# Up and gate projections as one Strassen-Winograd level over pairs of batches, in a fused gated-attention and ternary-FFN block

## The chip, the cores and the metric

The kernel runs on one core of one Trainium2 chip. The metric is device time in microseconds (us) of one execution. The kernel before takes 458.07 us (median of 3 runs, 457.31 to 458.22).

## What is computed

For each of 4 batches of 512 rows (model width 512): a layer norm of x is mixed by an attention matrix computed from a context of width 256, scaled by tanh of a gate and added to x; then a second layer norm feeds a gated FFN of width 2048 whose three weight matrices are made ternary.

```python
def ternary_quant(w):
    scale = jnp.mean(jnp.abs(w)) + EPS
    q = jnp.clip(jnp.round(w / scale), -1.0, 1.0) * scale
    return w + jax.lax.stop_gradient(q - w)
up = jnp.einsum('bsd,ed->bse', x, wu)          # wu, wg, wd: ternary
gate = jnp.einsum('bsd,ed->bse', x, wg)
hidden = jax.nn.silu(up) * gate
return jnp.einsum('bse,de->bsd', hidden, wd)
...
x = x + jnp.tanh(g_xattn[0]) * _L0_xattn_ref(_layernorm(x, axis=-1), ctx_1024, ...)
x = x + jnp.tanh(g_ffn[0]) * _L0_ffn_ref(_layernorm(x, axis=-1), W_up, W_gate, W_down)
```

## The kernel before, in words

One program drives six instruction streams, ordered by hand with semaphores. TensorE (`pe`), VectorE (`dve`), ScalarE (`act`), GpSimd (`pool`) and the DMA queue of SyncE (`sp`) each have a block; GpSimd also issues the loads of x.

**Attention, batches 0 to 3.** Per batch b: `project` (L303) makes q and k, `energy` (L312) the scores, the softmax runs on DVE and ACT, `transpose_p` (L322) turns the probabilities round, `mix` (L334, 8 fp32 matmuls a tile of 128 rows, 4 tiles) applies them, `make_x1` (L632) adds the result into x on DVE. Then `stats2`, `aggregate2`, a reciprocal root on GpSimd (`rstd2`, L256 and L259) and `norm_x1` (L647) give the second norm; `transpose_x` (L343) transposes it, ACT keeps the fp16 high part (`high_x`, L509), DVE the fp16 rest (`low_x`, L653). The stages of batch b+1 are interleaved with those of batch b by hand. Before the mix ACT adds a per-row shift to x (`shift_x`, L505).

**Weights.** `sum_abs` (L469) and `sum_abs_gate` (L474) on ACT sum the absolute values, `total` (L350) adds them over the partitions on PE, `weight_scale` (L661 to L667) on DVE makes the threshold; PE waits for it (`s_thr`) between batch 0 and batch 1. Two DVE operations make a piece ternary: `is_below` (L672) and `is_above_less` (L675). Up is done in batches 1 and 2 of the attention, gate and down tile by tile in the first FFN batch.

**FFN.** Batch after batch, over 16 tiles e of 128 hidden units. `up_gate` (L412 with the high part, L413 with the low) issues 2 x 4 x 2 = 16 matmuls of 128x512: up and gate, 4 blocks of the model width, high and low part. ACT makes silu (L579), DVE multiplies (`make_h`, L771), ACT takes the fp16 high part (L589), DVE the low (`low_h`, L776). `down` (L427, L428) issues 4 x 2 = 8 matmuls a tile, accumulating over e in four PSUM banks; L809 on DVE scales them, adds x, and `sp` stores. So the FFN is 4 x 16 x 16 = 1024 matmuls of up and gate and 4 x 16 x 8 = 512 of down.

```python
for k in range(KD):
    w = t_ug[:, ds(e * (KD * P) + (m * WCOLS + k * P), P)]
    pe.matmul(ps[par][:, :], w, hi[:, k, :], start=(k == 0), stop=False)
    last = pe.matmul(ps[par][:, :], w, lo[:, k, :], start=False, stop=(k == KD - 1))
```

## Time and profile before

| | |
|---|---|
| median of 3 runs | 458.07 us |
| the profiled execution | 458.36 us, its span 456.6 us |
| PE busy | 439.3 us (96% of the span), 1878 matmuls |
| DVE, ACT, POOL busy | 222.9, 162.4, 47.2 us |
| mean granted TensorE clock | 0.99 of full speed |

The span is from the first to the last instruction on the core. Matmuls are pipelined and the ends shown are modelled, so neighbouring matmuls overlap in the record: the distance from start to start is what one costs, not its duration. "Idle before" with a releaser names what an engine waited for. GpSimd is called POOL, TensorE PE, VectorE DVE, ScalarE ACT.

### The profile page before, as it was taken

How to read it: one execution, taken by the hardware profiler on the slowest of the kernel's cores; microseconds unless marked ns; L12 is line 12 of the kernel's file. 1: busy time of each engine (PE TensorE's matmuls, PEld its weight loads, DVE VectorE, ACT ScalarE, POOL GpSimd, SP SyncE). 2: the span in 40 equal slices, each digit the busy share in tenths (PEclk: the TensorE clock that was granted, in tenths of full speed). 3: DMA queues.
4: the chain of work that ended last, by engine and by line, in shares of the span. 5: the costliest groups of instructions: out<-in, count | busy, mean ns of one | idle time of the engine just before them, and what ended most of it. 6: DMA issues, size and time to landing. Idle time of an engine off the chain costs nothing.

```text
span 456.6 us, 6607 instructions
## 1 busy us (share of the span) xinstructions
PE 439.3 (96%) x1878; PEld 204.7 (45%) x1878; DVE 222.9 (49%) x384; ACT 162.4 (36%) x264; POOL 47.2 (10%) x115
## 2 busy tenths in 40 slices
PE   7995999999799999999999999999999999999996
PEld 5443444544344444444444444444444444444442
DVE  0576299998787767745222232422332252322224
ACT  2794577766522222222222222222222222222221
POOL 1225045446200000000000000000000000000000
PEclk9999899999989999999999999999999999999999
DMA  7997413332000000002000000200000011000002
GB/s 260 392 420 286 162 46 126 133 134 92 1 2 0 0 0 0 0 0 92 1 0 0 0 0 1 92 0 0 0 0 0 0 46 48 0 0 0 0 0 92
DMA packets 8445, 27.68 MB, mean 61 GB/s; under 512 B 1136, under 2 KB 1136, under 8 KB 6896
## 3 DMA queue, kind: packets, MB, share of 16 engines
q1 hardware_dynamic: 7344, 23.34, 13.8%
q0 software_dynamic: 1088, 4.19, 2.4%
q8 instruction: 5, 0.08, 0.1%
q14 instruction: 8, 0.07, 0.0%
...
## 4 chain that ended last, share of the span: by engine, by line
PE 85%; DVE 6%; issue 4%; POOL 2%; ACT 1%; DVEq 1%; POOLq 0%; ACTq 0%
PE bank L412 24%; PE bank L413 24%; PE bank L427 12%; PE bank L428 12%; PE bank L334 5%; PE bank L303 3%; PE bank L312 2%; POOL r L259 1%; DVE x_sb L632 1%; DVE st L637 1%; PE bank L322 1%; PE bank L355 1%; PE bank L343 1%; DVE t_ug L675 0%; DVE below L672 0%
## 5 line engine op out<-in xcount | busy, mean ns | idle before, releaser
L412 PE MATMUL bank<-xh,t_ug 128*128 128x512 f16 (+1 forms) x512 | 194.7, 380 | 0.0
L413 PE MATMUL bank<-xl,t_ug 128*128 128x512 f16 (+1 forms) x512 | 194.6, 380 | 0.0
L771 DVE SCALAR_TENSOR_TENSOR shared<-shared,kap,bank 128x512 f32<-128x512 f32 x64 | 47.8, 747 | 133.4 <-PE bank L413 133.2
L427 PE MATMUL bank<-shared 128*128 (+1 forms) x256 | 97.4, 381 | 3.0 <-DVE shared L776 3.0
L428 PE MATMUL bank<-shared 128*128 (+1 forms) x256 | 97.5, 381 | 0.0
L579 ACT ACTIVATE shared<-bank,su 128x512 f32<-128x512 f32 x64 | 44.0, 687 | 118.2 <-PE bank L413 118.2
L589 ACT ACTIVATE shared<-shared 128x512 f16<-128x512 f32 x64 | 40.3, 629 | 126.2 <-DVE shared L771 123.5
L412 PEld LDWEIGHTS bank<-xh,t_ug 128*128 (+1 forms) x512 | 50.3, 98 | 60.7 <-issue 1.0
L413 PEld LDWEIGHTS bank<-xl,t_ug 128*128 (+1 forms) x512 | 50.3, 98 | 60.6 <-issue 0.8
L776 DVE TENSOR_TENSOR shared<-shared 128x512 f16<-128x512 f32 x64 | 44.3, 692 | 54.0 <-ACT shared L589 54.0
L334 PE MATMUL bank<-shared,xt_sb 128*128 128x512 f32 (+1 forms) x128 | 57.5, 593 | 0.2 <-ACT shared L498 0.2
L427 PEld LDWEIGHTS bank<-shared 128*128 128x128 f16 x256 | 25.1, 98 | 33.4 <-DVE shared L675 3.0
L428 PEld LDWEIGHTS bank<-shared 128*128 128x128 f16 x256 | 25.1, 98 | 30.1 <-issue 0.3
L334 PEld LDWEIGHTS bank<-shared,xt_sb 128*128 128x128 f32 x128 | 23.3, 190 | 24.9 <-issue 23.9
L675 DVE SCALAR_TENSOR_TENSOR t_ug<-w_st,thr,below 128x512 bf16 (+2 forms) x24 | 22.3, 928 | 2.6 <-DVE below L672 2.2
L672 DVE TENSOR_SCALAR below<-w_st,nthr 128x512 bf16 (+2 forms) x40 | 21.4, 534 | 0.3 <-DVE nthr L667 0.2
L303 PE MATMUL bank<-shared,wqk 128*128 128x512 f32 x32 | 17.7, 687 | 2.8 <-DVE nthr L667 2.8
L612 DVE TENSOR_REDUCE nmax<-bank 128x1 f32<-128x512 f32 x16 | 11.0, 687 | 12.5 <-PE bank L312 12.4
L312 PE MATMUL bank<-shared 128*128 128x512 f32 x32 | 15.5, 596 | 0.8 <-ACT shared L481 0.8
L488 ACT ACTIVATE shared<-bank,nmax 128x512 f32<-128x512 f32 x16 | 11.0, 685 | 13.9 <-DVE nmax L612 13.6
L632 DVE SCALAR_TENSOR_TENSOR x_sb<-bank,tr,x_sb 128x512 f32<-128x512 f32 (+1 forms) x16 | 12.0, 747 | 8.0 <-PE bank L334 6.6
L653 DVE TENSOR_TENSOR xl<-bank,xh 128x512 f16<-128x512 f32 (+1 forms) x16 | 11.0, 688 | 8.1 <-ACT xh L509 7.8
...
## 6 DMA issues: line engine op xcount, KB each, us to landing
...
bqk_sb<-in_bqk SPq DMA_DIRECT2D x1, 1.0 KB, 3.3
```

The costliest lines, as they stand in the source:

```text
L303: last = pe.matmul((ps_q, ps_k)[m][:, :], wqk[:, c, m, :], ctx_sb[:, c * ROWS:(c + 1) * ROWS], start=(c == 0), stop=(c == NC - 1))
L312: pe.matmul(e_bank(b, i), q_sb[:, i * P:(i + 1) * P], k_sb, start=True, stop=True).then_inc(s_e, 1)
L334: last = pe.matmul(ps_x[i % 2][:, :], xt_sb[:, i, k, :], at[:, k, :], start=(k == 0), stop=(k == KD - 1))
L412: pe.matmul(ps[par][:, :], w, hi[:, k, :], start=(k == 0), stop=False)
L413: last = pe.matmul(ps[par][:, :], w, lo[:, k, :], start=False, stop=(k == KD - 1))
L427: pe.matmul(ps_o[j][:, :], hh[par][:, j * P:(j + 1) * P], w, start=first, stop=False)
L428: ins = pe.matmul(ps_o[j][:, :], hl[par][:, j * P:(j + 1) * P], w, start=False, stop=last)
L579: act.activation(a_sb[par], ps_up[par][:, :], ACT.Silu, scale=su[:, :]).then_inc(s_a, 1)
L589: act.activation(hh[par], h_sb[par], ACT.Copy).then_inc(s_hh, 1)
L675: dve.scalar_tensor_tensor(dst, w_st[:, ds(at, n)], thr[:, m:m + 1], tmp, ALU.is_gt, ALU.subtract).then_inc(done, 1)
L771: dve.scalar_tensor_tensor(h_sb[par], a_sb[par], kap[:, :], ps_gate[par][:, :], ALU.mult, ALU.mult).then_inc(s_h, 1)
L776: dve.tensor_tensor(hl[par], h_sb[par], hh[par], ALU.subtract).then_inc(s_hl, 1)
```

## The change

The 16 tiles of hidden units become 8 units of two tiles (rows 1 and 2 of a 2x2 block matrix A, whose columns are the two halves of the model width), for up and gate alike. The other factor B is a 2x2 block matrix too: its rows are the halves of the model width, its columns the two batches of a pair (0 and 1, then 2 and 3). `n` runs over 16 pairs of unit and batch pair. One Strassen-Winograd level replaces the eight block products by seven (`product1` to `product7`), each of 2 x 2 x 2 = 8 matmuls of 128x512, into PSUM pairs of banks (up beside gate).

- **Block sums of the weights** (S1 to S4, `unit_sums`) are made on POOL, four operations of 128x512 bf16 a unit. POOL also makes units 2 to 7 ternary (`unit_ternary`, three operations of 128x1024 for up and three for gate) and does the "below" half for units 0 and 1, whose other half is on DVE. The ternary values and the sums lie over the staged weights.
- **Block sums of the activations** (T1 to T4): the transposed norm is kept in fp32 (`xf`, `copy_x` in place of `high_x`/`low_x`), summed by operations of 128x1024 on DVE and POOL, and each of the seven blocks is then split in fp16 high (`high_t`, ACT) and low (`low_t`, DVE), 128x1024 at a time. For the second pair POOL makes the sums after the last unit of weights, and the splits are done in units 6 to 8.
- **Recombination**: a unit needs three copies from PSUM on ACT (`copy_1`, `copy_u2`, `copy_5`, 128x1024) and three adds on DVE (`add_11`, `add_12`, `add_22`, 128x1024); two of the products accumulate upon others in PSUM.
- **Down** (`down_half`, `expand`): from n = 3 to 14 one batch of one two-unit group is expanded between product 3 and product 7, 32 matmuls, with four evictions that add into x; the last four units (n = 12 to 15) close in eight banks at the end. There are 512 down matmuls as before, and 12 x 4 + 8 = 56 evictions of 128x512 where there were 16.
- **x of batches 2 and 3** is stored to a DRAM buffer after `make_x1` (8 stores), its place holds the ternary down weights, and it is loaded again over batches 0 and 1 once these are stored. Down weights are loaded twice (for the mean, then again in four pieces after the attention), and made ternary on DVE at n = 1, 3, 4 and 5 (`ternary_down`).
- **Attention**: `shift_x` leaves it (the shift is added on ACT at n = 4, 5, 12, 13); up's and gate's scale is computed together in batch 2, so that PE no longer waits for a threshold between batches 0 and 1; POOL's two small chains have the operations named above between them. x is loaded from the `sp` queue. The hardware loops are unrolled. `XS` goes from 2^10 to 2^8.

```diff
 @block.gpsimd
+            def unit_ternary(m, u):
...
+                pool.tensor_scalar(below[0][:, :], w_unit(m, u), nthr[:, m:m + 1], None, ALU.is_lt)\
+                    .then_inc(s_belp, 1)
+                pool.tensor_scalar(below[1][:, :], w_unit(m, u), thr[:, m:m + 1], None, ALU.is_gt)\
+                    .then_inc(s_belp, 1)
+                hold(pool, s_belp, 2 * k + 2)
+                pool.tensor_tensor(a_unit(m, u), below[1][:, :], below[0][:, :], ALU.subtract).then_inc(s_ternp, 1)
+            def unit_sums(u):
...
+                pool.tensor_tensor(a_blk(u, S1), a_blk(u, A21), a_blk(u, A22), ALU.add).then_inc(s_sum, 1)
+                hold(pool, s_sum, 4 * u + 1)
+                pool.tensor_tensor(a_blk(u, S2), a_blk(u, S1), a_blk(u, A11), ALU.subtract).then_inc(s_sum, 1)
+                hold(pool, s_sum, 4 * u + 2)
+                pool.tensor_tensor(a_blk(u, S4), a_blk(u, A12), a_blk(u, S2), ALU.subtract).then_inc(s_sum, 1)
+                pool.tensor_tensor(a_blk(u, S3), a_blk(u, A11), a_blk(u, A21), ALU.subtract).then_inc(s_sum, 1)
+            for b in range(NB):
                 for i in range(NT):
-                    rstd2(b, i, final=last and i == NT - 1)
+                    rstd2(b, i)
...
+                    if b == 2 and i in (1, 2):
+                        unit_below(i - 1, 0)
+                    if b == 3 and i == 0:
...
+                        pool.tensor_tensor(xf_half(0, 0), xf_half(1, 1), xf_half(0, 0), ALU.add).then_inc(s_t2, 1)
+                    if b == 3 and i == 1:
...
+                        pool.tensor_tensor(xf_half(0, 1), xf_half(0, 1), xf_half(0, 0), ALU.subtract).then_inc(s_t4, 1)
+                    if b == 3 and i == 2:
+                        unit_below(0, 1)
+                        unit_below(1, 1)
+            unit_sums(0)
+            unit_sums(1)
+            unit_ternary(0, 2)
+            unit_ternary(1, 2)
+            unit_sums(2)
...
+            for u in range(3, NU):
+                unit_ternary(0, u)
+                unit_ternary(1, u)
+                unit_sums(u)
...
 @block.tensor
+            def product(n, j, dst, a, blk, start):
...
+                for m in range(2):
+                    for k in range(2):
+                        w = a_unit(m, u) if a < 4 else wbf[:, m, u * 2 * UC + UC:(u + 1) * 2 * UC]
+                        o = (a % 4) * 256 + k * P
+                        pe.matmul(dst[:, m * 512:(m + 1) * 512], w[:, o:o + P], hi[:, k * 512:(k + 1) * 512],
+                                  start=start and k == 0, stop=False, skip_group_check=not start)
+                        last = pe.matmul(dst[:, m * 512:(m + 1) * 512], w[:, o:o + P], lo[:, k * 512:(k + 1) * 512],
+                                         start=False, stop=k == 1, skip_group_check=not start)
+            def product1(n):
+                if n < NU:
...
+                        pe.wait_ge(s_ternp, 2 * (n - 2) + 2)
...
+            for n in range(NN - 1):
+                product6(n)
+                product3(n)
...
+                if n >= 3:
+                    down_half(n)
+                product7(n)
+                product1(n + 1)
+                product2(n + 1)
+                product5(n + 1)
+                product4(n)
...
 @block.vector
+            for n in range(NN):
+                down = 3 <= n < NN - 1
+                low_h(n, "11")
+                if n > 0:
+                    make_h(n - 1, "21")
+                    low_h(n - 1, "21")
+                add_12(n)
+                if down:
+                    evict_half(n, 0)
+                make_h(n, "12")
...
+                low_h(n, "12")
+                add_22(n)
+                make_h(n, "22")
+                if n + 1 < NN:
+                    add_11(n + 1)
+                low_h(n, "22")
+                if n + 1 < NN:
+                    make_h(n + 1, "11")
```

On ACT, a unit is: `high_h(n, "11")`, `silu(n-1, "21")`, `copy_u2(n)`, `high_h(n-1, "21")`, `silu(n, "12")`, `high_h(n, "12")`, `silu(n, "22")`, `copy_1(n+1)`, `high_h(n, "22")`, `silu(n+1, "11")`, `copy_5(n+1)`. Product 6 waits for `copy_1`, product 3 for `copy_5`, product 7 for `copy_u2`; product 2 of the next unit waits for `add_11`, product 5 for `add_12`, product 4 for `add_22`.

## Rows read from the trace of the kernel before

**Rows 1.** The page: busy time, and POOL over 40 equal slices.
```profile
PE 439.3 (96%) x1878; PEld 204.7 (45%) x1878; DVE 222.9 (49%) x384; ACT 162.4 (36%) x264; POOL 47.2 (10%) x115
...
POOL 1225045446200000000000000000000000000000
```
**Rows 2.** Stages: length, busy us (x instructions) of each engine, clock, DMA share, GB/s.
```profile
39.70:44.50 4.80, 0.36 (x2) 0.30 (x2) 3.28 (x10) 1.61 (x2) 2.74 (x7) 1.00 0.61 227
44.50:92.00 47.50, 46.58 (x148) 23.05 (x148) 36.70 (x69) 32.50 (x62) 17.98 (x38) 0.96 0.35 116
92.00:113.90 21.90, 20.81 (x66) 10.14 (x67) 19.91 (x42) 13.50 (x21) 11.98 (x29) 1.00 0.30 109
113.90:130.40 16.50, 12.85 (x58) 6.02 (x57) 12.71 (x27) 7.55 (x11) 3.32 (x7) 0.90 0.00 0
130.40:453.00 322.60, 321.90 (x1492) 145.70 (x1490) 130.39 (x194) 81.62 (x124) 0.00 (x0) 1.00 0.03 10
```
**Rows 3.** Timeline of PE around its waits: start us, us, instruction, [idle before].
```profile
41.46 0.36 PE L350 MATMUL bank<-wabs,ones 128*128 128x4 f32 x2 [1.82 <-ACT t_ug L469]
44.56 3.51 PE L303 MATMUL bank<-shared,wqk 128*128 128x512 f32 x4 [2.75 <-DVE nthr L667]
...
113.94 0.38 PE L412 MATMUL bank<-xh,t_ug 128*128 128x512 f16 x1
...
125.84 0.38 PE L427 MATMUL bank<-shared 128*128 128x512 bf16 x1 [2.96 <-DVE shared L776]
```
**Rows 4.** FFN matmuls: groups of the page, and one later stage.
```profile
L412 PE MATMUL bank<-xh,t_ug 128*128 128x512 f16 (+1 forms) x512 | 194.7, 380 | 0.0
...
L427 PE MATMUL bank<-shared 128*128 (+1 forms) x256 | 97.4, 381 | 3.0 <-DVE shared L776 3.0
...
200.00:260.00 60.00, 60.00 (x279) 27.20 (x278) 19.90 (x28) 15.11 (x23) 0.00 (x0) 1.00 0.05 18
```
**Rows 5.** Groups by line and shape: busy us, mean ns of one, idle before.
```profile
L771 DVE SCALAR_TENSOR_TENSOR shared<-shared,kap,bank 128x512 f32<-128x512 f32 x64 | 47.8, 747 | 133.4 <-PE bank L413 133.2 <-issue 0.2
L776 DVE TENSOR_TENSOR shared<-shared 128x512 f16<-128x512 f32 x64 | 44.3, 692 | 54.0 <-ACT shared L589 54.0
L579 ACT ACTIVATE shared<-bank,su 128x512 f32<-128x512 f32 x64 | 44.0, 687 | 118.2 <-PE bank L413 118.2
L589 ACT ACTIVATE shared<-shared 128x512 f16<-128x512 f32 x64 | 40.3, 629 | 126.2 <-DVE shared L771 123.5 <-PE bank L428 2.7
L675 DVE SCALAR_TENSOR_TENSOR t_ug<-w_st,thr,below 128x1024 bf16 x8 | 10.2, 1279 | 0.0
L474 ACT ACTIVATE t_ug<-w_st x8 | 8.3, 1048 | 0.0
L469 ACT ACTIVATE t_ug<-w_st 128x2048 bf16<-128x2048 f32 x4 | 7.6, 1900 | 0.0
L672 DVE TENSOR_SCALAR below<-w_st,nthr 128x1024 bf16 x8 | 6.0, 747 | 0.0
```
**Rows 6.** Groups on POOL, by shape.
```profile
L226 POOL TENSOR_SCALAR_AFFINE_SELECT ident<-ident 128x128 f32<-128x128 f32 x1 | 0.3, 287 | 0.0
L285 POOL TENSOR_SCALAR kap<-scale 128x1 f32<-128x1 f32 x1 | 0.2, 190 | 0.0
```
**Rows 7.** Timeline of DVE (first row) and POOL: the same POOL operation beside it and alone.
```profile
60.15 1.28 DVE L675 SCALAR_TENSOR_TENSOR t_ug<-w_st,thr,below 128x1024 bf16 x1
...
60.78 0.69 POOL L247 TENSOR_TENSOR tr<-r,tanh_sb 128x1 f32<-128x1 f32 x1
61.65 0.26 POOL L249 TENSOR_SCALAR km<-mv,tr 128x1 f32<-128x1 f32 x1 [0.18 <-POOL tr L247]
...
79.04 0.19 POOL L247 TENSOR_TENSOR tr<-r,tanh_sb 128x1 f32<-128x1 f32 x1
```
**Rows 8.** Timeline of the end.
```profile
451.92 0.38 PE L428 MATMUL bank<-shared 128*128 128x512 bf16 x1
452.06 2.31 SPq L208 DMA_DIRECT2D out<-x_sb  x4
```

More of the change, by code:

```diff
@@ L315, in transpose_p @@
                 pe.wait_ge(s_pn, b * NT + i + 1)
[L316 removed]
+                if b > 0:
                     pe.wait_ge(s_at, b * NT + i)
@@ L363, in _ @@
                 transpose_p(0, i)
-            def attention(b, first=False, last=False):
+            for b in range(NB):
+                first, last = b == 0, b == NB - 1
                 if not (first or last):
@@ new lines, in product4, with expand @@
+            def product4(n):
+                pe.wait_ge(s_c["22"], n + 1)
+                product(n, 4, ps_c[n % 2], A22, "T4", False)
+            def expand(dst, units, b, i, first, last):
+                for n in units:
+                    for r in range(2):
+                        c = ("11", "21")[r] if b % 2 == 0 else ("12", "22")[r]
+                        pe.wait_ge(s_lo[c], n + 1)
+                        e = 2 * (n % NU) + r
+                        pe.wait_ge(s_td, e // 2 + 1)
+                        for lo in range(2):
+                            ins = pe.matmul(dst, h_part(n, c, lo)[:, i * P:(i + 1) * P], t_d[:, e * DM:(e + 1) * DM],
+                                            start=first and n == units[0] and r == 0 and lo == 0,
+                                            stop=last and n == units[-1] and r == 1 and lo == 1)
+                if last:
+                    ins.then_inc(s_dt, 1)
@@ L520, in _ @@
                 copy_at(0, i)
-            def attention(b, first=False, last=False):
+            for b in range(NB):
+                first, last = b == 0, b == NB - 1
                 if not last:
@@ L567, in _ @@
-            attention(0, first=True)
-            for c in range(NABS):
-                act.wait_ge(d_w[1][c], 16)
-            with act.Fori(1, NB - 1) as b:
-                attention(b)
-            attention(NB - 1, last=True)
-            high_x(NB - 1, NT - 2, NB * NT - 2)
-            def silu(b, e, par, head=False):
-                act.wait_ge(s_up, b * NE + e + 1)
-                if not head:
-                    act.wait_ge(s_h, b * NE + e - 1)
-                act.activation(a_sb[par], ps_up[par][:, :], ACT.Silu, scale=su[:, :]).then_inc(s_a, 1)
@@ L608, in _ @@
+            silu(NN - 1, "21")
+            high_h(NN - 1, "21")
         @block.vector
@@ L818 @@
+            make_h(NN - 1, "21")
+            low_h(NN - 1, "21")
+            for t in range(8):
+                b, i = (3, t) if t < 4 else (2, t - 4)
+                evict(4 * LAST_D + t, (bank[2:6] + [bank[0], bank[1], bank[6], bank[7]])[t], b, i)
 def kernel(x, ctx_1024, g_xattn, g_ffn, L0_xattn_Wq, L0_xattn_bq, L0_xattn_Wk, L0_xattn_bk,
```

1020 lines of the change are left out of this document (613 added, 407 removed).

## The prediction

> **What bounds the kernel now.** I read the page's busy line first: PE is busy 96% of the span, DVE 49%, ACT 36%, POOL 10% and over by the middle of the span [rows 1]. Then the table by stages, because the mean hides two different halves. From 130.4 to 453.0 us PE is busy 321.9 of 322.6 us at full clock, while DVE works 130 us and ACT 82; before that PE has small holes, and DVE is nearly full (19.9 of 21.9 us before the FFN) [rows 2]. So two thirds of the time is a stream of matmuls that waits for nobody, and only fewer matmuls shorten it. The durations shown for matmuls (380 ns) are modelled; 279 of them start in 60 us of a later stage, so one costs 60/279 = 0.215 us [rows 4]. There is something to win in the holes too: PE idles from 39.7 to 44.5 us for the first threshold, and waits 2.96 us at 122.9 us for the down weights [rows 2, 3]; the stage around that (16.5 us) has a granted clock of 0.90, about 1.6 us more.
>
> **Part 1, the matmuls.** Up and gate go from 1024 matmuls to 16 x 7 x 8 = 896; down keeps 512. 128 x 0.215 = **27.6 us** less, all on PE's path [rows 4]. One unit is 56 x 0.2155 = 12.1 us of PE, with half a down group (32 matmuls, 6.9 us) 19.0 us.
>
> **Part 2, the holes of the attention.** The 4.8 us stage goes, as nothing else in it was late for PE (ctx of batch 2 is loaded long before), and with it the slow clock behind it: 0.96 over 47.5 us is 1.9 us [rows 2, 3]. The down threshold is made in batch 3, which takes away the 2.96 us and the slow stretch behind it, 1.6 us [rows 2, 3]. What is late next: ACT. In batch 1 it gets eight pieces of work of its own: six sums of 128x2048 at 1.9 us where there were four of 1.05 [rows 5], and two splits of 128x1024 (about 1.05 us each), against four shifts that leave. That is 6 x 2.1 + 2.1 - 4 x 1.25 - 4 x 0.6 = 7.3 us more, on an engine that was busy 32.5 of 47.5 us [rows 2]: 16 of 24 us a batch become 23.6. Walking through the order, `copy_at` behind the sums reaches the transposes and the first mix of batch 2 about 3 us late. DVE is relieved in the same stages (eight pairs L672/L675 of 2.0 us leave it) [rows 5]. POOL's small chains now have large operations between them, and in batch 3 the roots of tiles 1 and 2 come behind one addition of 128x1024 each; DVE's `norm_x1` and with it `make_x1` of the last tile wait. I take 3 us (between 0 and 6). Sum: 4.8 + 1.9 + 3.0 + 1.6 - 3 - 3 = **5.3 us** less.
>
> Without any stall in the FFN that makes 458.4 - 27.6 - 5.3 = 425.5 us. The FFN's own small waits of before (0.7 and 0.6 us at the transposes, part of the 0.90 clock) also go: about 1.4 more, but the first unit has one of 1 us, for `product5(0)` needs the last root (3 us after the last mix) and then one sum on POOL. Base: **425 us**. The tail is as before: last matmul, one eviction, one store of 2.3 us [rows 8].
>
> **Part 3, the recombination: hidden if DVE and ACT are alone.** Per unit DVE gets three adds of 128x1024 from PSUM (1.28, by L675, the same form), four `make_h` (0.75), four `low_h` (0.69) and from n = 3 four evictions (0.75) [rows 5]: 9.6 and 12.6 us against 12.1 and 19.0 of PE. ACT gets three copies (1.05 by L474), four silu (0.69) and four copies (0.63): 8.4 us [rows 5]. The tightest link is `copy_u2`: product 7 waits for it, and in units without a down half only product 3 (1.72 us) lies between; 1.05 plus a wait fits. `make_h(n-1, "21")` must be done when the down half starts, 3.5 us after product 4 ended: silu 0.69 and 0.75 fit. So units 8 to 14, where POOL has no more work, should run as a closed stream. That is where half of the 27.6 us is safe. Unhidden are units 6 to 8, with seven more splits on ACT (1.05) and DVE (1.28) in the middle of the order: 2 us. The DRAM round trip of x has a unit of 19 us in between and costs PE nothing.
>
> **Part 4, POOL.** This is the open term. POOL has shown no large operation. Its work per unit 2 to 7 is four comparisons and two subtractions of 128x1024 and four sums of 128x512. Bounds: the 128x128 select took 287 ns and a 128x1 operation 190, so 0.8 ns an element in one pass [rows 6]. Lower end: every operation is one pass, 1.0 us for 1024 and 0.6 for 512: 8.4 us a unit. Upper end: two-input operations are three passes (2.65 and 1.4 us), comparisons two (1.8): 18.1. I take two passes for two inputs (1.8 and 1.0) and one for a comparison, nearest to the row: 4 x 1.0 + 2 x 1.8 + 4 x 1.0 = 11.6 us. Nine waits at 0.15 to 0.18 us [rows 7] make it 12.9.
>
> POOL also shares something with DVE: an operation on 128x1 took 0.69 us beside DVE's L675 (two SBUF inputs), ending 0.04 us after it, and 0.19 us alone [rows 7]. If the large ones behave so, POOL stands while DVE runs an operation with two SBUF inputs: `low_h` and three `make_h`, 5.0 us a unit, and 4.1 more (two pairs L672/L675) at n = 1, 3, 4 and 5.
>
> With product 1 of unit 0 at time 0 and POOL free at 3 us: sums of units 0 and 1 are done at 14.5; ternary of unit 2 at 28, while PE wants it at 24.3 (**late 4**); its sums 34.5, three small coefficients 36; ternary of unit 3 at 48, PE is there at 40 (**late 8**); unit 4 at 66 and PE at 67; later ones are ahead. Sum 12 us, and the clock: the two waits of the trace each cost 1.6 to 1.9 us of slow clock [rows 2], so 2 us more. DVE waits for POOL in turn; if it waits half a POOL operation (0.5 us) at each of 7 to 11 shared operations, units 3 to 5 have 16.7 + 5 us of DVE against 19 of PE, less 1.5 us by which neighbouring DVE operations overlap: 5 us. Part 4: **19 us**. With 2 us of part 3: 425 + 21 = 446; but the waits of PE in units 2 and 3 give DVE and ACT back the time in which they are late, so I take off 3: **443 us**, 3.3% under the median of 458.07 (the sum stands on the profiled 458.36, 0.3 us higher).
>
> The Trainium skill bears on this in two places, which the sum does not use. "SBUF — State Buffer" (Who interferes with whom) says that the port pair shared by VectorE and GpSimd is an exclusive lock for the whole instruction; the 0.69 us beside DVE agrees for one direction, the other no row shows. "GPSIMD Engine Reference" (Elementwise — side-by-side cycle accounting) gives 4497 ns for a two-input add of 2048 fp32, so an estimate of 2.3 us for 1024; with it the lateness of unit 3 would be some 16 instead of 12 us and the time about 450. It speaks against putting this work on POOL.
>
> **Rivals.**
> *Everything hidden.* POOL makes its operations in one pass (9.7 us a unit with waits), and DVE does not disturb it: unit 2 is ready at 19, before 24.3, and nothing is late. 425 + 2 = 427, or 421 if the attention gives back its 6 us too. For it: 0.8 ns an element [rows 6]. Against it: two inputs, and rows 7.
> *Slower: POOL is the pace of the first half.* Its place are units 2 to 7, its price the upper end: 18.1 + 1.3 + about 7 us of DVE's shared operations = 26.4 us a unit against 19.0. Then unit 2 is 11 us late, unit 3 27, unit 4 33, units 5 to 7 7.4 each more: 55 us; 425 + 55 + 2 + 3 = 485. It decides from 33 us of stalls (458 - 425), which is a POOL unit of some 17 us before DVE's share. For it: PE, DVE and POOL are coupled by one order, and a late comparison delays seven products. A milder one (20 us a unit) gives 463.
> *The links inside a unit.* If silu, multiply, split and add run in each other's way so that each of 16 units loses 0.7 us, the second half shows it too: 443 + 11 = 454. For it: DVE has 9.6 of 12.1 us in units 0 to 2; against it: 12.6 of 19.0 later.
>
> **How the numbers follow.** The forecast (431 to 453) 0.48; everything hidden (below 431) 0.19; links (453 to 457.1) 0.06; slower by POOL 0.24; what is left, 0.03, is no change. A difference of 0.2% (0.9 us) is about what a measurement of this kernel can tell from none. Faster by more: 0.48 + 0.19 + 0.06 = 0.73, minus 0.01 for the edge: 0.72; within: 0.04; slower: 0.24. The time is that of the likeliest case, 443; the range for 8 in 10 is 422 to 467: it takes in the lower case and the milder slower one, and leaves out the 485. The forecast's own range is 431 to 453.
>
> **What would show it.** L412's successors: 896 matmuls; from unit 8 on PE full, with units of 19.0 us. Right in part 4: PE waits for POOL before product 1 of units 2 and 3, none later; POOL's 128x1024 subtractions near 1.8 us, sums near 1.0. Wrong: PE waiting for POOL at every unit to 7 (slower), or never (hidden). Right in part 2: no wait of 2.75 us between batches 0 and 1, first FFN matmul near 113 us (113.9 before); wrong if it starts after 117 or before 109. If PE waits for DVE or ACT in units 9 to 14, part 3 is wrong. DVE's operations with two SBUF inputs longer than 1.28 and 0.69 us beside POOL would show the coupling in the other direction.

## The result, and the profile after

The kernel after takes 483.03 us (median of 4 runs, 481.19 to 483.66) against 458.14 us (457.31 to 458.49, 4 runs): a ratio of 1.054, 95% interval 1.051 to 1.057. The profiled execution is one of 483.66 us, its span 481.8. The prediction was 443, range 422 to 467, and wrong in sign.

The page of the kernel after: busy time, POOL over 40 slices, granted clock, and the groups of POOL's large operations and of DVE's operations with two SBUF inputs (busy us, mean ns of one, idle before).

```profile
PE 424.2 (88%) x1733; PEld 193.2 (40%) x1748; DVE 314.3 (65%) x408; ACT 218.1 (45%) x318; POOL 217.1 (45%) x189
...
POOL 0233354878999999999999952000000000000000
PEclk9999999998698869979797999999999999999999
...
L1031 DVE SCALAR_TENSOR_TENSOR xf<-xf,small 128x512 f32<-128x512 f32 x48 | 41.9, 872 | 22.8 <-ACT xf L792 22.2
L1036 DVE TENSOR_TENSOR sh<-xf,sh 128x512 f16<-128x512 f32 x48 | 38.2, 797 | 14.6 <-ACT sh L798 14.5
...
L343 POOL TENSOR_SCALAR below<-w_sb,small 128x1024 bf16<-128x1024 f32 x12 | 36.5, 3043 | 1.0 <-POOL w_sb L348 1.0
L345 POOL TENSOR_SCALAR below<-w_sb,small 128x1024 bf16<-128x1024 f32 x12 | 35.5, 2958 | 0.0
...
L348 POOL TENSOR_TENSOR w_sb<-below 128x1024 bf16<-128x1024 bf16 x12 | 27.4, 2286 | 1.8
```

POOL, over by the middle of the span and 10% busy before [rows 1], is a row of nines from the 11th to the 23rd slice, and PE's clock has its gaps in the same slices. A comparison takes 3.0 us, a subtraction 2.3. The stages of the kernel after (length, busy us and instructions of PE, PEld, DVE, ACT and POOL, clock, DMA share, GB/s):

```profile
39.70:44.50 4.80, 4.80 (x18) 2.51 (x18) 2.45 (x6) 2.83 (x7) 2.30 (x7) 1.00 0.80 284
...
109.00:130.40 21.40, 10.88 (x44) 5.16 (x45) 15.17 (x19) 4.91 (x6) 19.50 (x17) 0.76 0.22 74
130.40:200.00 69.60, 53.53 (x216) 22.21 (x215) 48.73 (x47) 27.29 (x38) 66.87 (x33) 0.88 0.05 16
200.00:260.00 60.00, 44.83 (x178) 18.39 (x181) 46.33 (x43) 20.77 (x30) 57.77 (x27) 0.87 0.10 36
260.00:320.00 60.00, 57.43 (x254) 25.18 (x256) 44.65 (x51) 30.05 (x40) 25.41 (x12) 0.96 0.00 1
320.00:380.00 60.00, 59.84 (x277) 27.20 (x278) 38.67 (x48) 24.49 (x35) 0.00 (x0) 1.00 0.21 71
```

The second half is what was forecast: PE full, 277 matmuls in 60 us. In the first half POOL is busy 144.1 of 151.0 us (109.0 to 260.0), while PE stands still for a quarter of it and issues at a lower clock. The stage of the old threshold wait (39.7 to 44.5), where PE had 0.36 us of work [rows 2], is full now.

The waits of PE that cost most, from its timeline (start us, us, instruction, [idle before <- what ended it]):

```profile
123.62 0.58 PE L524 MATMUL pair<-xb_hi,w_sb 128*128 128x512 f16 x1 [10.27 <-issue]
124.00 0.63 PE L526 MATMUL pair<-xb_lo,w_sb 128*128 128x512 f16 x1
124.43 0.63 PE L524 MATMUL pair<-xb_hi,w_sb 128*128 128x512 f16 x1
...
151.08 0.39 PE L524 MATMUL pair<-xb_hi,w_sb 128*128 128x512 f16 x1 [2.38 <-POOL w_sb L348]
...
176.72 0.61 PE L524 MATMUL pair<-xb_hi,w_sb 128*128 128x512 f16 x1 [7.27 <-POOL w_sb L348]
...
204.28 0.59 PE L524 MATMUL pair<-xb_hi,w_sb 128*128 128x512 f16 x1 [5.60 <-DVE x_sb L1066]
...
232.79 0.59 PE L524 MATMUL pair<-xb_hi,w_sb 128*128 128x512 f16 x1 [5.03 <-DVE x_sb L1066]
```

Three different causes stand here. At 123.62 us it is product 5 of the first unit, which waits for its block sum (POOL ends it at 123.52). At 151.08 and 176.72 us it is product 1 of units 2 and 3, whose weights are not yet ternary. At 204.28 and 232.79 us it is product 1 of n = 4 and 5, and at 258.65 us that of n = 6 (4.45 us), which wait for an eviction on DVE; POOL had made their weights ternary 5.5, 9.9 and 12.2 us before. Behind the waits of 10.27, 7.27 and 5.03 us the granted clock is 0.50, and matmuls start 0.43 us apart instead of 0.215, the lower of the two clock levels (1.2 GHz).

**Losses by unit.** I take the start of each unit's second product (of the first product for n = 0) from the timeline, and subtract the unit's length without stalls (12.1 us for n < 3, 19.0 later). The starts are 109.7, 135.8, 153.9, 180.1, 207.7, 236.2, 262.0, 282.2, 303.9, 322.9, so the losses of n = 0 to 7 are 14.0, 6.0, 14.1, 8.6, 9.5, 6.8, 1.2 and 2.7: 62.9 us, and nothing later. Without them the kernel would take 109.7 + 3 x 12.1 + 12 x 19.0 + 44.9 (unit 15 to the end of the span) + 1.9 = 420.8 us. The waits over 0.25 us in these units add up to 43.8 us; the other 19 are the lower clock behind them, smaller gaps, and some 1.4 us of two transposes that stand in unit 0.

### The profile page after: what moved, and what is told of

Same layout as the page of the kernel before. It is cut to its first block, busy times and chain, and to the rows that moved or that the text cites. A ratio compares the mean times of both kernels' runs of the same rounds, so it can differ in the third digit from the quotient of the medians.

```text
span 481.8 us, 5521 instructions
## 1 busy us (share of the span) xinstructions
PE 424.2 (88%) x1733; PEld 193.2 (40%) x1748; DVE 314.3 (65%) x408; ACT 218.1 (45%) x318; POOL 217.1 (45%) x189
## 4 chain that ended last, share of the span: by engine, by line
PE 62%; POOL 16%; DVE 9%; issue 8%; ACT 4%; DMA 1%; POOLq 0%; DVEq 0%; ACTq 0%
PE pair L595 19%; PE pair L524 15%; PE pair L526 15%; PE pair L453 6%; PE pair L423 3%; POOL below L343 2%; POOL below L345 2%; POOL w_sb L348 2%; POOL below L333 2%; PE pair L432 2%; DVE t_tmp L1050 2%; DVE x_sb L1052 1%; DVE x_sb L1066 1%; POOL small L324 1%; DMA sh<-in_ctxT 1%
## 5 line engine op out<-in xcount | busy, mean ns | idle before, releaser
L524 PE MATMUL pair<-xb_hi,w_sb 128*128 128x512 f16 x448 | 179.3, 400 | 42.8 <-DVE x_sb L1066 15.1
L526 PE MATMUL pair<-xb_lo,w_sb 128*128 128x512 f16 x448 | 178.9, 399 | 0.0
L595 PE MATMUL pair<-x_sb,sh 128*128 128x512 bf16 x497 | 110.6, 379 | 3.5 <-DVE x_sb L1066 1.6
L524 PEld LDWEIGHTS pair<-xb_hi,w_sb 128*128 128x128 bf16 x448 | 45.8, 102 | 105.4 <-issue 38.7
L595 PEld LDWEIGHTS pair<-x_sb,sh 128*128 128x128 f16 x512 | 49.5, 98 | 64.4 <-DVE x_sb L1066 4.6
L526 PEld LDWEIGHTS pair<-xb_lo,w_sb 128*128 128x128 bf16 x448 | 45.6, 102 | 56.7 <-issue 9.8
L1066 DVE SCALAR_TENSOR_TENSOR x_sb<-pair,small,x_sb 128x512 f32<-128x512 f32 x56 | 41.8, 747 | 32.6 <-PE pair L595 31.5
L453 PE MATMUL pair<-sh,xt_sb 128*128 128x512 f32 x128 | 57.5, 593 | 0.1
L1031 DVE SCALAR_TENSOR_TENSOR xf<-xf,small 128x512 f32<-128x512 f32 x48 | 41.9, 872 | 22.8 <-ACT xf L792 22.2
L1036 DVE TENSOR_TENSOR sh<-xf,sh 128x512 f16<-128x512 f32 x48 | 38.2, 797 | 14.6 <-ACT sh L798 14.5
L343 POOL TENSOR_SCALAR below<-w_sb,small 128x1024 bf16<-128x1024 f32 x12 | 36.5, 3043 | 1.0 <-POOL w_sb L348 1.0
L345 POOL TENSOR_SCALAR below<-w_sb,small 128x1024 bf16<-128x1024 f32 x12 | 35.5, 2958 | 0.0
L1036 DVE TENSOR_TENSOR sh<-c,sh 128x512 f16<-128x512 f32 x16 | 14.1, 882 | 21.8 <-ACT sh L798 21.8
```

What stands on the lines that cost most here:

```text
L343: pool.tensor_scalar(below[0][:, :], w_unit(m, u), nthr[:, m:m + 1], None, ALU.is_lt)\
L345: pool.tensor_scalar(below[1][:, :], w_unit(m, u), thr[:, m:m + 1], None, ALU.is_gt)\
L453: last = pe.matmul(ps_x[i % 2], xt_tile(i)[:, k, :], at[:, k, :], start=(k == 0), stop=(k == KD - 1))
L524: pe.matmul(dst[:, m * 512:(m + 1) * 512], w[:, o:o + P], hi[:, k * 512:(k + 1) * 512], start=start and k == 0, stop=False, skip_group_che ...
L526: last = pe.matmul(dst[:, m * 512:(m + 1) * 512], w[:, o:o + P], lo[:, k * 512:(k + 1) * 512], start=False, stop=k == 1, skip_group_check= ...
L595: ins = pe.matmul(dst, h_part(n, c, lo)[:, i * P:(i + 1) * P], t_d[:, e * DM:(e + 1) * DM], start=first and n == units[0] and r == 0 and l ...
```

## The experiments

Losses of n = 0 to 7 in the same manner, for the kernels that matter below (the first four compute everything, the last three leave POOL's weight operations out):

| kernel | us | losses of n = 0 to 7 | sum |
|---|---|---|---|
| after | 483.0 | 14.0, 6.0, 14.1, 8.6, 9.5, 6.8, 1.2, 2.7 | 62.9 |
| h1_fast_ternary | 473.8 | 14.0, 1.4, 11.1, 10.4, 7.5, 4.6, 1.3, 2.7 | 53.0 |
| f4_all_mended | 465.5 | 14.2, 0, 7.7, 8.6, 4.7, 0.5, 0.4, 9.9 | 46.0 |
| f5_sums_on_dve | 462.0 | 14.5, 0, 7.5, 8.6, 4.8, 0.4, 0.5, 5.6 | 41.9 |
| e1_pool_free | 450.9 | 11.1, 0, 4.9, 4.6, 3.7, 4.7, 0, 2.6 | 31.6 |
| k1_pool_free_mended | 447.9 | 12.0, 0, 2.1, 2.9, 0.5, 0.4, 0.5, 11.4 | 29.8 |
| k2_floor_sums_on_dve | 443.2 | 11.8, 0, 2.1, 2.9, 0.4, 0.5, 0.4, 5.7 | 23.8 |

### POOL's weight operations taken away

```diff
-pool.tensor_scalar(below[0][:, :], w_unit(m, u), nthr[:, m:m + 1], None, ALU.is_lt)
-pool.tensor_scalar(below[1][:, :], w_unit(m, u), thr[:, m:m + 1], None, ALU.is_gt)
-pool.tensor_tensor(a_unit(m, u), below[1][:, :], below[0][:, :], ALU.subtract)
+pool.memset(w_unit(m, u), 0.0)
...
-(the four block sums of a unit)
+pool.memset(a_blk(u, blk), 0.0)  # u < 2, a nop for the others
```

> Leaves out GpSimd's work on the up and gate weights: its comparisons, subtractions and block sums are replaced by memsets of zeros over the same places (one of 128x1024 fp32 for a unit and matrix, four small ones for units 0 and 1); all of PE, ACT and DVE stays. Theory P (POOL's work, by its own length and by what it does to DVE beside it, is what makes the changed kernel slow): the first FFN product stays near 109 us, then 1408 x 0.2155 = 303 us follow nearly closed, plus a few us in units 0 and 6 to 8 and 4 us of tail: 418 to 428 us. Theory R (the recombination chain of ACT and DVE, with 120 us more of DVE and ACT work, costs PE by itself): PE's waits in the first half stay at more than half of their 65 us: 450 to 470 us.

Measured: 450.94 us (450.33 to 451.83), ratio 0.987 (0.985 to 0.989). POOL's weight work costs 32 us: the losses halve, from 62.9 to 31.6, and the first FFN matmul starts 2.2 us earlier (107.5). Theory P (418 to 428) is refuted as the whole cause; the time lies at the lower end of theory R's range.

### Is it POOL's lateness, or what POOL reads?

```diff
-(the two comparisons)
+for r in range(6): pool.memset(below[r // 3][:, :], 0.0)   # each with its wait
```

> GpSimd's two comparisons of each unit and matrix (units 2 to 7), 2.9 us each beside DVE, are each replaced by three write-only memsets of 128x1024 bf16 with a wait behind each (about 3 x 0.95 + 0.2 us); the result of the comparison is left out. So POOL is as late as before, but reads nothing for two thirds of its time. Theory P1 (POOL's lateness is the cost): PE still gets a unit each 22 us or later, 470 to 482 us. Theory P2 (POOL's reads stop DVE's operations with two SBUF inputs and the chain evict, product 1 pays): DVE's operations go back to 0.75 and 0.69 us, PE's waits for evictions go, only those for POOL in units 2 and 3 stay: 450 to 462 us.

Measured: 485.52 us, ratio 1.062 (1.060 to 1.064). Six memsets of 0.96 us, which read nothing, cost as much as two comparisons of 3.0. It is above the ranges of both theories (470 to 482 and 450 to 462). So it is not the reading of the comparisons that costs. The run does not part POOL's time from its reading altogether: it leaves the comparisons out, but keeps subtraction and sums, which read, and these are what POOL does beside DVE's down weights in n = 3 and 4. The four operations in front of the last eviction of n = 4 take 1.78, 1.99, 1.45 and 1.98 us here, as long as in the kernel after (below).

### The down weights' ternary on DVE taken away

```diff
-dve.tensor_scalar(t_tmp, part, nthr[:, 2:3], None, ALU.is_lt)
-dve.scalar_tensor_tensor(t_d[...], part, thr[:, 2:3], t_tmp, ALU.is_gt, ALU.subtract)
+dve.memset(x_sb[:, o:o + 512], 0.0)
```

> Leaves out the ternary form of the down weights on DVE at n = 1, 3, 4 and 5 (eight pairs of 1.3 and 2.0 us in the changed kernel), memsets of 128x512 fp32 stand in its place. Theory P1: POOL paces the first half, its unit still takes 20.2 us of operations and waits, DVE was only late because it had time: 475 to 483 us (POOL is disturbed a little less). Theory P2 (DVE paces units 3 to 5): the 5 us waits of product 1 of units 4, 5 and 6 for the last eviction go: 463 to 470 us.

Measured: 473.2 us, ratio 1.035 (1.032 to 1.037); the down weights are left out. This is between the two theories. The waits for an eviction in n = 3 to 5 are gone, and waits of 3.2, 3.0 and 0.7 us for POOL appear in their place; the one for POOL at unit 3 grows from 7.3 to 9.3 us, and unit 7 loses 9.9 us instead of 2.7. So behind DVE's block POOL is the next limit of these units. In the kernel after, DVE's timeline shows the mechanism: between the third and the last eviction of n = 4 stand four operations, stretched by POOL, and product 1 of n = 5 starts 0.88 us after that last eviction began.

```profile
223.35 1.40 DVE L1066 SCALAR_TENSOR_TENSOR x_sb<-pair,small,x_sb 128x512 f32<-128x512 f32 x2
224.67 1.61 DVE L1050 TENSOR_SCALAR t_tmp<-xt_sb,small 128x1024 bf16<-128x1024 f32 x1
226.38 1.99 DVE L1052 SCALAR_TENSOR_TENSOR x_sb<-xt_sb,small,t_tmp 128x1024 bf16<-128x1024 f32 x1
228.48 1.45 DVE L1050 TENSOR_SCALAR t_tmp<-xt_sb,small 128x1024 bf16<-128x1024 f32 x1
230.03 1.95 DVE L1052 SCALAR_TENSOR_TENSOR x_sb<-xt_sb,small,t_tmp 128x1024 bf16<-128x1024 f32 x1
231.91 0.74 DVE L1066 SCALAR_TENSOR_TENSOR x_sb<-pair,small,x_sb 128x512 f32<-128x512 f32 x1
```

### POOL's prices by themselves

A kernel of single operations (POOL alone, then ten DVE operations beside four pairs of POOL's); it computes nothing of the reference.

> Computes nothing of the block; it measures single operations. First GpSimd alone, each operation twice with a wait behind it: if the comparison of 128x1024 fp32 is slow by itself it takes 2.8 us alone, and if its output type or the comparison is the reason, multiply and add or minimum and maximum on the same tile take 0.9 to 1.5 us; if every pass over fp32 costs that, they take 2.8 too. The two-input bf16 subtraction 2.1 us, 512 columns 1.15. Then GpSimd comparisons and two-input subtractions beside one kind of DVE operation at a time. Theory P2: DVE's operation with two SBUF inputs and its fp32 tensor_scalar (0.75 alone) are stretched by up to a whole GpSimd operation, the one with a PSUM and one SBUF input is not; beside GpSimd memsets the two-input one is not stretched.

Groups of POOL: L129 is the comparison beside DVE and L48 the same alone, L111 one with a constant, L60 and L66 two-input operations, L96 and L84 multiply and add.

```profile
L129 POOL TENSOR_SCALAR B<-xs,thr 128x1024 bf16<-128x1024 f32 x4 | 14.8, 3696 | 1.4 <-DVE D L176 0.9 <-POOL F L132 0.5
...
L48 POOL TENSOR_SCALAR B<-xs,thr 128x1024 bf16<-128x1024 f32 x1 | 2.8, 2844 | 4.5 <-DVE D L174 4.5
...
L111 POOL TENSOR_SCALAR B<-xs 128x1024 bf16<-128x1024 f32 x1 | 2.8, 2767 | 0.2 <-POOL B L108 0.2
...
L60 POOL TENSOR_TENSOR B<-B 128x1024 bf16<-128x1024 bf16 x1 | 2.1, 2114 | 0.1
...
L66 POOL TENSOR_TENSOR B<-B 128x512 bf16<-128x512 bf16 x1 | 1.1, 1148 | 0.1
...
L96 POOL TENSOR_SCALAR F<-xs,thr 128x1024 f32<-128x1024 f32 x1 | 1.1, 1118 | 0.2 <-POOL F L93 0.2
...
L84 POOL TENSOR_SCALAR F<-xs 128x1024 f32<-128x1024 f32 x1 | 1.0, 1044 | 0.2 <-POOL F L81 0.2
```

Groups of DVE: x10 beside POOL's comparison and two-input operation, x8 beside its memsets, x1 alone.

```profile
L179 DVE SCALAR_TENSOR_TENSOR D<-xs,thr,D 128x1024 bf16<-128x1024 f32 x10 | 20.5, 2051 | 1.0
L186 DVE TENSOR_SCALAR D<-xs,thr 128x1024 bf16<-128x1024 f32 x10 | 17.8, 1776 | 1.1
L193 DVE TENSOR_TENSOR D<-ps,xs 128x1024 bf16<-128x1024 f32 x10 | 12.3, 1225 | 1.0
L200 DVE SCALAR_TENSOR_TENSOR D<-xs,thr,D 128x1024 bf16<-128x1024 f32 x8 | 10.3, 1284 | 0.8
L165 DVE SCALAR_TENSOR_TENSOR D<-xs,thr,D 128x1024 bf16<-128x1024 f32 x1 | 1.3, 1285 | 12.5 <-POOL thr L44 12.5
L168 DVE TENSOR_SCALAR D<-xs,thr 128x1024 bf16<-128x1024 f32 x1 | 0.8, 753 | 0.1
```

A comparison is 2.84 us, but multiply and add (L84, L96) 1.04 to 1.12. Both engines stretch: POOL's comparison from 2.84 to 3.70, DVE's two-input operation from 1.28 to 2.05, its fp32 one-input operation from 0.75 to 1.78. DVE's operation with one operand in PSUM stays at 1.23, and POOL's memsets do not stretch the two-input operation (the only one run beside them).

### Another arithmetic on POOL

The prices suggest rounding by adding a large constant in place of comparing. Two versions: the first uses subtract with min, and max with multiply.

```diff
+pool.tensor_scalar(w_unit(m, u), w_unit(m, u), inv[:, m:m + 1], RND, ALU.mult, ALU.add)
+pool.tensor_scalar(below[0][:, :], w_unit(m, u), RND, 1.0, ALU.subtract, ALU.min)
+pool.tensor_scalar(a_unit(m, u), below[0][:, :], -1.0, 1.0, ALU.max, ALU.mult)
```

> One part changed: GpSimd makes a piece of units 2 to 7 ternary without comparisons, in three arithmetic passes (times 1/scale plus 1.5 x 2^23, which rounds; minus it and min 1; max -1), by the single-operation run 1.12 + 1.04 + 1.04 us with 0.17 us waits, where two comparisons and a subtraction took 2.84 + 2.84 + 2.11. A unit on POOL falls from 20.2 to about 12.6 us of operations and waits, 17 us beside DVE: no longer the pace. What is left is what the run with POOL freed left. Theory P and D together: 451 to 458 us. If POOL's length was not what mattered (only its contention, which stays), 470 or more.

Measured: 485.76 us, ratio 1.061 (1.059 to 1.063), a miss: in this trace the first pass takes 1.19 us, the others 3.70 and 3.83. For subtract with min only the pair can be the reason, as min with max took 1.04 us in m1 with the same input and output types; the pass with max and multiply also has another input type (bf16). The second version keeps to the pairs measured fast:

```diff
+pool.tensor_scalar(w_unit(m, u), w_unit(m, u), inv[:, m:m + 1], RND, ALU.mult, ALU.add)
+pool.tensor_scalar(w_unit(m, u), w_unit(m, u), RND + 1.0, RND - 1.0, ALU.min, ALU.max)
+pool.tensor_scalar(a_unit(m, u), w_unit(m, u), 1.0, -RND, ALU.mult, ALU.add)
```

> One part changed against the changed kernel: the ternary form of units 2 to 7 on POOL in three passes that use only operation pairs measured at 1.04 to 1.12 us for 128x1024 by themselves (multiply and add; min and max; multiply and add), where the earlier arithmetic form had two pairs (subtract and min; max and multiply) that took 3.9 and 3.7 us. POOL's unit then is 2 x 3.7 + 4.6 + 0.6 = 12.6 us before DVE's share, about 17 with it. Theory P: POOL is no longer the pace, and what stays is near the run with POOL freed (451): 451 to 459 us. If POOL's contention and not its length is the cost: 470 or more.

Measured: 473.79 us (473.33 to 475.05), ratio 1.035 (1.033 to 1.037). The passes take 1.47, 1.20 and 1.32 us; POOL's twelve weight blocks start from 135.9 to 214.0 us, 14.2 us a unit instead of 23.1 (134.4 to 261.3). The gain is 9 us, well short of the 32 of e1, and the time lies in the range given for "contention and not length" (470 or more). POOL's unit is now near the 12.9 us of the prediction, and the kernel still takes 31 us more than predicted. The 7.27 us wait for POOL's weights at unit 3 is gone, but in n = 2 PE waits 8.13 us for DVE's `add_22`: DVE stays stretched, as its groups from 130 to 235 us show (`make_h` and `low_h`, 0.75 and 0.69 without POOL [rows 5]).

```profile
L1036 DVE SCALAR_TENSOR_TENSOR xf<-xf,small 128x512 f32<-128x512 f32 x15 | 15.5, 1033 | 8.1 <-ACT xf L797 8.1
L1041 DVE TENSOR_TENSOR sh<-xf,sh 128x512 f16<-128x512 f32 x15 | 14.9, 990 | 5.4 <-ACT sh L803 5.4
```

### The order on DVE, and the first unit

g2_down_spread makes the down weights ternary piece by piece over n = 1 to 6 instead of two at once; f2 joins it with f1's arithmetic, and f3 adds a first attempt at the first unit (T2 and T4 a tile later, the below halves of units 0 and 1 on DVE).

> One part changed: the eight pieces of the ternary down weights on DVE are spread one by one over n = 1 to 6 (two at n = 3 and 6, the second one behind add_11), in place of pairs at n = 1, 3, 4, 5 in front of the last eviction; POOL as in the changed kernel. Theory D alone (DVE's block in front of the eviction is the cost of units 3 to 5): 463 to 468 us. Theory P and D together, as in the run without this work: POOL takes over as the pace, 472 to 479 us.

> Both parts: arithmetic ternary on POOL and the down pieces spread on DVE. Theory P and D together: the gain is larger than the sum of the two alone, since each hides the other; waits of product 1 for evictions and for POOL go, those in the first unit and at units 7 and 8 (about 10 and 3 us) stay: 436 to 444 us. If the links inside a unit cost (theory R): above 450.

> As the run before, and the start of the FFN mended: DVE makes the 'below' half of units 0 and 1 itself (POOL needed 2.9 us for each of four), and POOL's two additions for T2 and T4 come one tile later in batch 3, where its chains of reciprocal roots have room; the splits of T2 and T4 follow them. The 10 us wait of product 5 of unit 0 for the first block sum falls to 1 to 4 us: 6 to 9 us under the run before, 428 to 437 us. If that wait comes from DVE's or ACT's load at the end of the attention and not from POOL, within 2 us of the run before.

Measured: 480.28 (ratio 1.049, 1.047 to 1.051), 485.8 and 482.4 us. f2 and f3 carry f1's slow passes and are more than 40 us above their ranges. Spreading alone gives 3 us, less than either theory gave: the waits in n = 3 to 5 shrink, but n = 7 loses 10.6 us instead of 2.7 (units start at 271.1 and 300.7).

f4_all_mended is h1's arithmetic, the spreading, T2 and T4 and the below halves of units 0 and 1 on DVE, and the first unit's S1 and S2 ahead of the last root.

> All mended together: the fast ternary form on POOL, the down pieces spread over n = 1 to 6 on DVE, units 0 and 1 and the sums T2 and T4 on DVE, and the first two block sums of unit 0 before the last reciprocal root. Theory P and D: no wait over 3 us is left but one at n = 7; 1408 x 0.2155 = 303 us of FFN after a first product near 107 us, plus 8 to 15 us of small waits and 4 us of tail: 424 to 436 us, under the kernel before (458). If the recombination itself costs (theory R), units 1 to 7 still lose 2 to 4 us each: 440 to 450.

Measured: 465.5 us (464.93 to 468.16), ratio 1.019 (1.015 to 1.023). Far above what I expected. Unit 0 loses as much as before, by other links. Product 5 waits 3.5 us for `make_x1` of the last tile, which stands behind the sum for T4 on DVE; the block sum S1 was done 3.1 us before. Then a transpose waits 4.6 us for a copy on ACT; the copy stands behind a silu, the silu waits 6.3 us for `add_11`, and that stands behind four ternary operations of unit 1 on DVE (119.47 to 124.55 us). And n = 7 loses 9.9.

### What is left without POOL, and unit 7

k1 is f4 with POOL's weight operations replaced by memsets, as in e1: the ternary values of units 2 to 7 and the block sums are left out.

> The kernel after with the four amendments of f4_all_mended (down weights made ternary piece by piece over units 1 to 6, the below halves of units 0 and 1 and the sums T2 and T4 on DVE, the first unit's sums before the last root), and with POOL's weight operations replaced by memsets of the same regions: ternary values and block sums of the weights are left out. It is to show what is left of the 28 us by which e1_pool_free (450.9) stands above the 425 of the sum. Theory R (those 28 us are the down weights' ternary in front of the eviction that product 1 waits for, 11 us of waits in units 4 to 6, the 7.4 us wait of the first unit and the slow clock behind each): 431 to 437 us. Rival S (the recombination itself does not fit beside PE even when DVE is not stretched): above 443.

Measured: 447.89 us (446.92 to 448.83), ratio 0.977 (0.974 to 0.980). Theory R (431 to 437) fell: only 3 us less than e1. The time is in the range of rival S (above 443), but 11.4 us of it is a new loss that the spreading makes in unit 7. Theory R's part about the down weights holds (n = 3 to 5 lose 3.8 us instead of 13.0), but unit 0 is no better (the same two waits as in f4, 1.7 and 5.1 us). The timeline of DVE in k1:

```profile
244.08 2.84 DVE L1028 SCALAR_TENSOR_TENSOR xf<-xf,small 128x512 f32<-128x512 f32 x1
246.84 6.64 DVE L940 TENSOR_TENSOR xb_lo<-xf,xb_hi 128x1024 f16<-128x1024 f32 x2
```

That of POOL beside it, and then that of PE:

```profile
243.71 2.66 POOL L396 TENSOR_TENSOR xt_sb<-xf 128x1024 f32<-128x1024 f32 x1 [105.27 <-DVE x_sb L1049]
246.51 2.60 POOL L398 TENSOR_TENSOR xf<-xf 128x1024 f32<-128x1024 f32 x1
249.08 3.32 POOL L399 TENSOR_TENSOR xt_sb<-xt_sb,xf 128x1024 f32<-128x1024 f32 x1
```

```profile
254.79 1.46 PE L583 MATMUL pair<-x_sb,sh 128*128 128x512 bf16 x3 [7.74 <-DVE c L1028]
```

`make_h` ends 0.55 us behind POOL's first addition, and two splits take 6.64 us beside the next two. The spreading had moved the last ternary piece to n = 6, and POOL's sums for the second pair, which wait for it, into unit 7. The next runs have these four sums made by DVE:

```diff
-pool.tensor_tensor(tmp[0], xf_half(3, 1), xf_half(3, 0), ALU.subtract)   # and three more
+dve.tensor_tensor(tmp[0], xf_half(3, 1), xf_half(3, 0), ALU.subtract)    # n = 7, three more in n = 7 and 8
```

> k1_pool_free_mended (447.9, ternary values and block sums of the weights left out) with the four block sums of the second batch pair (128x1024 fp32, 2.6 to 3.3 us each on POOL) made by DVE in units 7 and 8. Theory T (the 7.74 us wait at the down half of unit 7 and the slow clock behind it come from these four POOL operations, in which make_h took 2.84 us instead of 0.74 and two splits 6.64 instead of 2.36): POOL has no work there, DVE's operations go back to 0.74 and 1.22 us, and the time is 436 to 440. Rival U (the unit is late because DVE has 20 us of work in it, whoever makes the sums): 445 to 449.

> f4_all_mended (465.5, nothing left out) with the same edit: the four sums of the second pair on DVE. Theory T: 453 to 458, as much less as in the other run. Rival U: 463 to 467.

Measured: 443.16 us (ratio 0.967, 0.965 to 0.968) and 461.97 us (ratio 1.009, 1.007 to 1.011). The same operations of DVE in k2, and PE's wait behind them:

```profile
245.26 0.75 DVE L1018 SCALAR_TENSOR_TENSOR xf<-xf,small 128x512 f32<-128x512 f32 x1
245.92 2.35 DVE L930 TENSOR_TENSOR xb_lo<-xf,xb_hi 128x1024 f16<-128x1024 f32 x2
```

```profile
249.59 3.63 PE L573 MATMUL pair<-x_sb,sh 128*128 128x512 bf16 x16 [1.36 <-DVE c L1018]
```

Theory T names the wait rightly (7.74 us becomes 1.36), but the gain is half of what it gave in k2 (4.7 us), and 3.5 us in f5, which stays above its range (453 to 458): DVE's own sums now stand before the evictions, and PE waits 0.76, 1.69 and 1.14 us there. So T and U each hold in part: 5.7 us in unit 7 belong to POOL's additions, 5.7 to the amount of work. Both depend on the place: in e1, where the last ternary piece is at n = 5, POOL makes the same sums and unit 7 loses 2.6.

### Taking two of POOL's three passes away

```diff
+act.activation(w_unit(m, u), w_unit(m, u), ACT.Identity, scale=inv[:, m:m + 1], bias=rnd_p[:, :])
+pool.tensor_scalar(w_unit(m, u), w_unit(m, u), RND + 1.0, RND - 1.0, ALU.min, ALU.max)
+act.activation(a_unit(m, u), w_unit(m, u), ACT.Identity, bias=rnd_m[:, :])
```

> f5_sums_on_dve with the three passes that make the weights of units 2 to 7 ternary shared out: ACT makes the first (multiply and add the rounding constant) and the last (subtract it, to bf16), POOL only the clamp between them; nothing is left out. POOL's unit goes from some 14 to 8 us and stretches DVE for less of the time; ACT gets 4 x 1.05 us a unit more. If POOL's share of the port is what still costs time in units 2 to 5 (f4's units are 17.6 us longer than those of k1): 446 to 452. If ACT, which sits in the links inside a unit, becomes late in units 0 to 2: 455 to 465.

Measured: 463.29 us (462.38 to 464.01), ratio 1.011 (1.009 to 1.012). The time lies in the range for "ACT becomes late" (455 to 465); what POOL's hold on DVE still costs it does not tell. From 130.4 to 200.0 us (as in the stages above)

```profile
130.40:200.00 69.60, 57.63 (x240) 23.49 (x239) 46.84 (x51) 43.16 (x54) 29.20 (x26) 0.94 0.05 16
```

POOL is busy 29.2 us (f5: 63.3) and DVE 46.8 (f5: 56.6), so POOL's hold on DVE is less: from 136 to 235 us the ternary operation of the down weights falls from 1.85 to 1.43 us, while `make_h` stays at 1.04. But ACT has 43.2 us (f5: 29.2), and its passes of 1.1 to 1.2 us come before the copies that the next product waits for: waits for ACT of 2.4 us in n = 1 and n = 2, which f5 has not. One wait was turned into another.

### Part 2 by itself

The kernel before, with up's total and threshold made in batch 1 and its eight ternary pieces on later tiles; the loop over batches 1 and 2 unrolled.

```diff
+if b == 1 and i == 0:
+    pe.wait_ge(s_qk, 5)
+    total(0, NABS, ps_q)
-pe.wait_ge(s_qk, 3)
-total(0, NABS, ps_q)
-pe.wait_ge(s_thr, 1)
-with pe.Fori(1, NB - 1) as b:
-    attention(b)
+attention(1)
+pe.wait_ge(s_thr, 1)
+attention(2)
```

> The kernel before, with the one part of the change that needs no Strassen level: the total and the threshold of the up weights are made after the first mix of batch 1 instead of between batches 0 and 1, its eight ternary pieces go to the batches' later tiles, and the loop over batches 1 and 2 is unrolled. If part 2 of the sum is right for this stall (4.8 us of idle PE and 1.9 us of slow clock, less what comes late behind it): 452 to 455 us, ratio 0.988 to 0.993. If the time of the stall is given back at once because DVE and ACT set the pace of the attention: 456.5 to 458.5.

Measured: 453.72 us (453.13 to 453.88) against 458.4, ratio 0.990 (0.988 to 0.993). It is the fastest of the kernels that compute everything. Its first FFN matmul:

```profile
109.42 0.38 PE L413 MATMUL bank<-xh,t_ug 128*128 128x512 f16 x1
```

Before it was at 113.94 [rows 3]: 4.5 us earlier, as much as the median gained.

## Why the prediction was wrong

**The step that failed is part 4.** It put POOL's cost mainly into waits for POOL's weights (12 us of the 19). These waits came, and were shorter (9.7 us). What was mis-sized is what POOL and the order of the operations do to everything else. The losses of n = 0 to 5 (59.0 us), by what ended the waits over 0.25 us:

| part of the loss | in the sum | measured, us |
|---|---|---|
| product 1 of units 2 and 3 waits for POOL | 12 | 9.7 |
| waits for DVE (evictions 16.4, `add_22` 2.6) | 5 | 18.9 |
| product 5 of the first unit | 1 (in the base) | 10.3 |
| waits for copies on ACT | 0 | 2.5 |
| lower clock, smaller gaps, transposes | 2 | 17.7 |

The sum also took 3 us off, for waits that overlap.

**The price of a comparison** was wrong too. The text set POOL's one-input operation at 1.0 us, comparisons included ("one for a comparison, nearest to the row"), from a select and a one-column operation [rows 6]. A comparison is 2.84 us alone and 3.0 here, three times that, and above even the upper end (1.8). Four of them make 12.0 us of a unit that I took for 12.9 in all and that is 23.1. The two-input operation (1.8 taken, upper end 2.65) is 2.29 and the sums (1.0 taken) 1.26 to 1.58. But this price by itself explains only a part: h1 brings POOL's unit to 14.2 us and gains 9 of the 40 us by which the prediction was off. The estimate of 2.3 us that stood beside the sum, from the Trainium skill's "GPSIMD Engine Reference" (Elementwise — side-by-side cycle accounting), is what m1's trace shows for the two-input operation in fp32 (2.34 alone); for the comparison no estimate stood there.

**Which rival happened?** "POOL is the pace of the first half" was priced at 485 (483 measured), and its point of decision was right: it needed 33 us of stalls and there were 63. Its mechanism happened only in part, so that the two numbers agree is largely luck: it put all 55 us on POOL, and e1 gives POOL 30 of the 59. Its sign, PE waiting for POOL at every unit to 7, did not come; the one that did is the sign written down for the forecast, waits for POOL before product 1 of units 2 and 3 and none later. From n = 4 on POOL's weights lie ready and DVE's evictions are late. By the runs, from 443 to the profiled 483.7:

- Base 420.8 instead of 425. Part 1 stands: units without a stall take 19.0 us, n = 8 to 14 to the tenth. Part 2 gave more than it was set at: the first FFN matmul is at 109.7, not near 113. b1 alone, which has only the first of its edits, gives 4.5 us there, against 6.7 less what comes late.
- Part 3 is right in the second half. Units 6 and 7 lose 3.9 us where 2 stood.
- The rest, the term of part 4 (19, with 3 taken off), is 59.0 us in n = 0 to 5. e1 has 29.0 there, so POOL's weight work is 30 of them. Of e1's 29, some 9 are the down weights' ternary in front of the eviction (n = 3 to 5: 13.0 in e1, 3.8 in k1). I had counted these operations in DVE's load, but not their place in the order. Another 11 are the first unit. The last 9 are n = 2 (4.9) and what k1 keeps in n = 3 to 5 (3.8).

**The first unit** was given one wait of 1 us. It is 10.3: the last root came behind two comparisons of 3.0 us each on POOL. But e1 still waits 7.4 us there and loses 11.1 in the unit. The edits of the order in f3, f4 and k1 leave 17.2, 14.2 and 12.0 us in this unit, against 14.0. Behind the root stand the links that f4 and k1 show, `make_x1` of the last tile and unit 1's ternary operations in front of `add_11`; no run has all three out of the way, so what the unit would then lose is open.

**The coupling of POOL and DVE** was in the prediction, with the lock cited from "SBUF — State Buffer" (Who interferes with whom) in the Trainium skill. The runs show the direction that no row showed: DVE's operations stretch too (1.28 to 2.05 us in m1, 0.74 to 2.84 in k1). An operation with one operand in PSUM is not stretched (1.23 us beside POOL and alone). I charged DVE 0.5 us at each of 7 to 11 operations, in total 5 us. What stays in n = 2 to 5 between f5 (21.3 us) and k2 (5.9 us) is 15 us, in which POOL still has 14.2 us of work a unit. f6 was to tell how much of that is the stretching and how much waiting for weights, and did not; f5's own trace says more. From n = 0 on it has no wait of PE over 0.25 us that POOL ends. Those of n = 2 to 5 add up to 14.8 us, and DVE ends all of them. The longest, in n = 2 (DVE, then PE):

```profile
147.29 1.54 DVE L1031 SCALAR_TENSOR_TENSOR xf<-xf,small 128x512 f32<-128x512 f32 x1 [0.86 <-ACT xf L781]
148.76 1.53 DVE L1050 TENSOR_SCALAR t_tmp<-xt_sb,small 128x1024 bf16<-128x1024 f32 x1
150.39 1.94 DVE L1052 SCALAR_TENSOR_TENSOR x_sb<-xt_sb,small,t_tmp 128x1024 bf16<-128x1024 f32 x1
152.26 1.52 DVE L1036 TENSOR_TENSOR sh<-xf,sh 128x512 f16<-128x512 f32 x1
```

```profile
154.97 0.61 PE L515 MATMUL pair<-xb_hi,w_sb 128*128 128x512 f16 x1 [4.37 <-DVE xf L1026]
```

In k2, without POOL's work, the same four take 0.75, 0.75, 1.28 and 0.69 us, and PE waits 0.34 us there. So in this place the stretching is the cause, 3.1 of the 4.0 us.

**The rival of the links** inside a unit is refuted for n = 8 to 14, where PE never waits. In n = 2 to 5 the kernels without POOL's weight work (k1, k2) still lose 5.9 us.
